# GpSimd's order in the steady passes: a k*v product ahead of the first sum, behind a wait for the gated attention rows

## The chip, the core and the metric

The kernel runs on one core of a Trainium2 chip. The metric is device time in microseconds (us), median over runs. The core has TensorE (matrix products), VectorE, ScalarE and GpSimd (elementwise work, each with its own queue of instructions), and SyncE, which here only issues transfers. The engines wait for each other by semaphores.

## What is computed

Two layers follow one another. The first is a cross-attention over 64 sequences of 64 channels and 256 steps, with a batch normalisation. The second is a recurrent layer (time mixing with a per-channel state, then channel mixing). The change lies in the second. Its core, cut short:

```python
xn = _ln(x, ln1_w, ln1_b)
sx = _token_shift(xn, state[:, i1])
x5 = xn[:, :, None] + sx[:, :, None] * (maa_stack + xxx)     # five mixed inputs
w = jnp.exp(-jnp.exp(time_decay + jnp.tanh(x5[:, :, 1] @ decay_w1) @ decay_w2))
r, k, v = x5[:, :, 3] @ Wr.T, x5[:, :, 0] @ Wk.T, x5[:, :, 2] @ Wv.T
g = jax.nn.silu(x5[:, :, 4] @ Wg.T)
def step(s, rkvw):                       # 64 steps, per head an 8 x 8 state
    a = k_t[:, :, :, None] * v_t[:, :, None, :]
    out = jnp.einsum('bhk,bhkd->bhd', r_t, u * a + s)
    return (a + w_t[:, :, :, None] * s, out)
x = x + (groupnorm(att) * gn_w + gn_b) * g @ Wo.T
xn2 = _ln(x, ln2_w, ln2_b); sx2 = _token_shift(xn2, state[:, i0])
kk = jnp.square(jax.nn.relu((xn2 + sx2 * ffn_maa_k) @ ffn_Wk.T))
x = x + jax.nn.sigmoid((xn2 + sx2 * ffn_maa_r) @ ffn_Wr.T) * (kk @ ffn_Wv.T)
```

## The kernel before

Everything is float32. The second layer works through 8 chunks (`CHUNKS`) of 8 sequences, 512 tokens each. Each engine has its own program, written out by hand; a pass of an engine is a call of its `body(n, p)`. A steady pass `n` does three things at once: the late part of chunk n-1 (`c_...`: group norm, output projection, second layernorm, channel mixing), the state part of chunk n (`b_...`) and the early part of chunk n+1 (`a_...`: shift, mixed inputs, projections). Before the steady passes 1 to 6 lie a filling and a first pass, behind them a last pass and a draining one. Passes 1 to 4 are a loop of two bodies (an odd and an even one) whose semaphore values come from registers. Passes 5 and 6 are written out with constants, and pass 6 has no `z_add`.

The state part handles two halves of the channels (h = 0, 1), each in two parts (q = 0, 1) of 512 x 4 columns. For each (h, q):
- k*v (`b_kv`) is formed in the state buffer `st[q]`: by GpSimd for (0, 0), (0, 1) and (1, 0) (L656), by VectorE for (1, 1) (L1446). It reads `vb[h]`, into which SyncE has spread v by eight transfers (L601).
- VectorE runs four scans over it (L1459, decay `w` in PSUM) and then the product with r (L1464), which writes over `vb` and frees `st[q]`. TensorE sums the product up (L858).

Buffers `st[0]` and `st[1]` take turns, so the k*v of (1, 0) can start as soon as the product of (0, 0) is done (semaphore `prod_ready`).

The mixed inputs go through three engines: TensorE makes the modulation (L816, L821), VectorE multiplies it by the shift into `x5` (`a_mod`, L1419), and GpSimd adds xn (`add_x(n + 1, j)`, L683). Then TensorE projects: j = 0 feeds the decay (`a_dec1`, L830 and L832), j = 1 the values (L793 on `ps_a`), j = 2, 3, 4 the keys, receptances and gates. `add_x` waits for the second channel half of its modulation (`mod_ready`).

VectorE's steady pass, as far as it matters here: scans and product of (0, 0), bonus and shift, the group norm of chunk n-1 (`c_gn`: L1523 twice, then the gated rows `ag`, L1527 twice, each of which raises `ag_ready`), the modulations 0 and 1 (L1419 four times), scans and product of (0, 1), the moments of x1 (`c_x1`, L1391 to L1397), scans and product of (1, 0), the second shift with the key mix (`c_shift`, L1537, L1541), further modulations and the k*v of (1, 1), scans and product of (1, 1), and the output gate (L1551).

GpSimd's steady pass: first tokens (`prev`), `add_x` 0, k*v (1, 0), `z_add` (a transfer from memory that adds, L662), `add_x` 1, a square root of the second layernorm (`rstd`, L638, L640), `add_x` 2 and 3, `rstd` of the first layernorm, k*v (0, 0) of the next chunk, `add_x` 4, k*v (0, 1), and the output's transfer (L669).

Of the kernel before, what the change touches and what calls it, by code (L numbers as in the profile page):

```python
# [46 lines left out]
def wait(eng, sem, value):  # L47

    if isinstance(value, int) and value <= 0:
        return  # L50
    eng.wait_ge(sem, value)
# [374 lines left out]
def rwkv(nc, sem, t, d, out):  # L426
# [30 lines left out]
    att_copied, att_sq, var_ln, gn_rstd, gn_scaled, ag_ready = sem("att_copied"), sem("att_squared"), sem("var_ln"), sem("gn_rstd"), sem("att_scaled"), sem("att_gated")  # L457
# [40 lines left out]
    with ctx:  # L498
# [57 lines left out]
        def wide(ap):  # L556

            return bt(ap).rearrange("p b (a t) -> p a b t", a=1).broadcast_to([P, 4, NB, L])
# [15 lines left out]
        def kv_at(n, h, q):  # L574

            if (h, q) in KV_BY_POOL:
                return kv_pool, n * len(KV_BY_POOL) + KV_BY_POOL.index((h, q)) + 1
            return kv_vector, n * len(KV_BY_VECTOR) + KV_BY_VECTOR.index((h, q)) + 1
# [56 lines left out]
        def _(pool):  # L635
            def rstd(n, var_sem, sem_out, src, dst):
                pool.wait_ge(var_sem, n * 2 + 2)
                nc.gpsimd.tensor_tensor(dst[:, 0, :], src[:, 0, :], t["mhalf"][:, :], ALU.pow).then_inc(sem_out, 1)  # L638
                pool.wait_ge(sem_out, n * 2 + 1)
                nc.gpsimd.tensor_tensor(dst[:, 1, :], src[:, 1, :], dst[:, 0, :], ALU.mult).then_inc(sem_out, 1)  # L640

            def prev(n, shift_sem, sem_out, src, dst):

                wait(pool, shift_sem, n)
                for c in range(EC):
                    nc.gpsimd.tensor_copy(dst[:, NB * c:NB * c + NB, 0], src[:, c, bass.ds(n * NB, NB)]).then_inc(sem_out, 1)  # L646

            def b_kv(n, p, h, q):

                pool.wait_ge(v_spread[h], n * 16 * S + 16 * S)  # L650
                pool.wait_ge(k_ready, n * 2 + h + 1)
                src = vb[h][:, q:S:2, :].rearrange("p e (b t) -> p e b t", t=L)
                wait(pool, prod_ready, n * 4 + 2 * h + q - 1)
                if isinstance(n, int) and n == 0 and (h, q) == (0, 1):
                    pool.wait_ge(kv_pool, 1)
                nc.gpsimd.tensor_tensor(st[q][:, :, :, 1:L], src[:, :, :, 0:L - 1], wide(k[p][h][:, :])[:, :, :, 0:L - 1],  # L656
                                        ALU.mult).then_inc(kv_at(n, h, q)[0], 1)

            def z_add(n):

                pool.wait_ge(x_biased, n)
                pool.dma_start(wyz[:, bass.ds(n * TILES, TILES), :], d["x"][bass.ds(n * TILES, TILES)].rearrange("a p f -> p a f"),  # L662
                               accum_op=ALU.add).then_inc(z_ready, 16)

            def add_out(n):

                pool.wait_ge(y_mid, n * 2 + 4)
                pool.wait_ge(x1_stored, n * 16 + 16)
                pool.dma_start(out[bass.ds(n * TILES, TILES)].rearrange("a p f -> p a f"), y, accum_op=ALU.add).then_inc(stored, 16)  # L669

            def last_rstd2(i):
# [3 lines left out]
                pool.wait_ge(last_ln, 2 * i + 1)  # L675
                nc.gpsimd.tensor_tensor(rs2[:, 1, cut], ve2[:, 1, cut], rs2[:, 0, cut], ALU.mult).then_inc(last_ln, 1)

            def hold(n):
                pool.wait_ge(bonus_ready, n * 2 + 2)

            def add_x(n, j):
                pool.wait_ge(mod_ready, n * 10 + MOD_ORDER.index(f"w{j}b") + 1)
                nc.gpsimd.tensor_tensor(x5[j % 2][:, :, :], x5[j % 2][:, :, :], xn[:, :, 1:L1], ALU.add).then_inc(x5_ready, 1)  # L683
# [8 lines left out]
            def first_pass(n, p):  # L692
                q = 1 - p
                prev(n + 1, sx_ready, xprev, t["prev1"], xn)
                hold(n)
                b_kv(n, p, 1, 0)
                add_x(n + 1, 0)
                add_x(n + 1, 1)
                z_add(n + 2)
                add_x(n + 1, 2)  # L700
                add_x(n + 1, 3)
                b_kv(n + 1, q, 0, 0)
                add_x(n + 1, 4)
                rstd(n + 2, ln1_var, ln1_rstd, ve1, rs1)
                b_kv(n + 1, q, 0, 1)

            def body(n, p, z=True):
                q = 1 - p
                prev(n - 1, sx2_ready, xprev2, t["prev0"], xn2)
                prev(n + 1, sx_ready, xprev, t["prev1"], xn)  # L710
                add_x(n + 1, 0)
                b_kv(n, p, 1, 0)
                if z:
                    z_add(n + 2)
                add_x(n + 1, 1)
                rstd(n - 1, ln2_var, ln2_rstd, ve2, rs2)
                add_x(n + 1, 2)
                add_x(n + 1, 3)
                if z:
                    rstd(n + 2, ln1_var, ln1_rstd, ve1, rs1)  # L720
                b_kv(n + 1, q, 0, 0)
                add_x(n + 1, 4)
                b_kv(n + 1, q, 0, 1)
                add_out(n - 1)
# [23 lines left out]
            with pool.Fori(1, CHUNKS - 4, 2) as n:  # L748
                body(n, 1)
                body(n + 1, 0)  # L750
            body(CHUNKS - 3, 1)
            body(CHUNKS - 2, 0, z=False)
            last_pass(CHUNKS - 1, 1)
# [1020 lines left out]
```

## Time and profile before

| | us |
|---|---|
| median of 3 runs | 692.4 (690.88 to 697.16) |
| the profiled execution, its own time | 689.89 |
| its span, first to last instruction | 688.0 |
| TensorE busy (matrix products) | 613.5 (89%) |
| VectorE busy | 574.1 (83%) |
| ScalarE busy | 390.5 (57%) |
| GpSimd busy | 294.1 (43%) |
| chain that ended last: PE, DVE, issue, POOL | 29%, 17%, 11%, 7% |

In the profile TensorE is called PE (PEld its weight loads), VectorE DVE, ScalarE ACT, GpSimd POOL and SyncE SP; POOLq is GpSimd's sequencer. All times in rows are microseconds from the start of the span unless marked ns. Busy time is an average over the attention layer (up to about 150 us), the passes and the ends. The steady passes run from about 270 to 626 us.

### The profile page before, as it was taken

To read this page: it belongs to the slowest core of one execution; us is meant where nothing else is said; L and a number is where in the kernel's file an instruction comes from. 1 tells how busy PE (TensorE), PEld (TensorE's weight loads), DVE (VectorE), ACT (ScalarE), POOL (GpSimd) and SP (SyncE) were. 2 spreads that over 40 slices of the span, in tenths; PEclk is the share of its full clock that TensorE was granted. 3 is DMA by queue.
4 is the path that set the end of the run, shared out by engine and by line. 5 is a ranking of instruction groups with operands and counts; after the bars stand their busy time and mean duration, and the time that the engine had idled before them with its cause. 6 is when DMAs were issued, how large, how long until landed. Compare 5 with 4: busy or idle time off the path is not lost.

```text
span 688.0 us, 9610 instructions
## 1 busy us (share of the span) xinstructions
PE 613.5 (89%) x2694; PEld 332.2 (48%) x2694; DVE 574.1 (83%) x902; ACT 390.5 (57%) x933; POOL 294.1 (43%) x210
## 2 busy tenths in 40 slices
PE   8999999979787859899899989989988998995896
PEld 5666666647232224354445435344543534443475
DVE  2999999973568898978997997899799789959944
ACT  3888888853443354567365455737546464353343
POOL 1111363002035293475639428464851946590020
PEclk9999999999999999999999999999999999998699
DMA  2343222201270841456267055526706540670020
GB/s 68 121 124 105 83 72 61 83 13 31 77 168 0 154 92 31 80 135 124 31 153 143 10 106 131 99 30 152 152 4 127 131 74 4 149 153 30 0 31 30
DMA packets 42444, 57.87 MB, mean 84 GB/s; under 512 B 4978, under 2 KB 25106, under 8 KB 42418
## 3 DMA queue, kind: packets, MB, share of 16 engines
q1 hardware_dynamic: 33008, 46.77, 29.6%
q0 software_dynamic: 9104, 10.77, 8.9%
q8 instruction: 11, 0.18, 0.1%
q14 instruction: 15, 0.12, 0.1%
q10 hardware_dynamic: 306, 0.02, 0.0%
HBM read 16.13 MB, written 7.86 MB: 35 GB/s over the span
## 4 chain that ended last, share of the span: by engine, by line
PE 29%; DVE 17%; issue 11%; POOL 7%; ACT 4%; DMA 1%; SPq 1%; DVEq 0%; POOLq 0%; ACTq 0%
PE ps_a L793 9%; DVE state L1459 8%; PE ps_c L878 6%; PE ps_c L793 3%; POOL x L683 2%; POOL state L656 2%; DVE vb L1464 2%; PE ps_att L858 2%; DVE x L1419 2%; PE ps_a L816 1%; PE ps_a L821 1%; DVE sx L1537 1%; DMA vb<-v 1%; PE ps_c L931 1%; POOL xn L646 1%
## 5 line engine op out<-in xcount | busy, mean ns | idle before, releaser
L683 POOL TENSOR_TENSOR x<-x,xn 128x1024 f32<-128x1024 f32 x35 | 86.2, 2471 | 151.0 <-DVE x L1419 151.0
L1459 DVE TENSOR_TENSOR_SCAN state<-ps_w,state 128x512 f32<-128x512 f32 x128 | 145.8, 1200 | 0.2
L793 PE MATMUL ps_a<-x,wsq 128*128 128x512 f32 x256 | 119.3, 610 | 10.1 <-POOL x L683 7.5
L656 POOL TENSOR_TENSOR state<-vb,k 128x2016 f32<-128x2016 f32 x23 | 105.3, 4577 | 27.0 <-DVE state L1446 10.4
L1464 DVE TENSOR_TENSOR vb<-state,r 128x2048 f32<-128x2048 f32 x32 | 86.1, 2692 | 1.7
L793 PEld LDWEIGHTS ps_a<-x,wsq 128*128 128x128 f32 x256 | 48.5, 195 | 68.9 <-issue 59.4
L1419 DVE SCALAR_TENSOR_TENSOR x<-ps_a,vec,sx 128x512 f32<-128x512 f32 x80 | 56.2, 745 | 27.7 <-PE ps_a L816 15.9
L310 ACT ACTIVATE probs<-ps_f,negmax 128x256 f32<-128x256 f32 x128 | 59.0, 473 | 1.9 <-DVE negmax L364 1.1
L816 PE MATMUL ps_a<-mix_t,w 64*128 64x512 f32 x128 | 47.6, 634 | 9.8 <-ACT mix_t L1161 7.1
L1117 ACT ACTIVATE zn<-wyz,rs 128x256 f32 (+1 forms) x60 | 31.1, 594 | 22.5 <-POOL rs L640 22.5
L374 DVE TENSOR_SCALAR probs<-probs,rowinv 128x256 f32<-128x256 f32 x128 | 41.8, 369 | 2.2
L1213 ACT ACTIVATE wyz<-ps_c 128x512 f32 (+1 forms) x14 | 8.4, 597 | 60.0 <-PE ps_c L892 60.0
L858 PE MATMUL ps_att<-vb,pick 128*32 128x512 f32 x256 | 35.0, 619 | 8.3 <-DVE vb L1464 8.3
L364 DVE TENSOR_REDUCE negmax<-ps_f 128x2 f32<-128x512 f32 x64 | 40.9, 681 | 0.9 <-PE ps_f L226 0.9
L249 PE MATMUL ps_av<-probsT,gz 128*64 128x256 f32 x256 | 34.7, 388 | 3.8 <-issue 2.4
L226 PE MATMUL ps_f<-thph 32*128 32x256 f32 x256 | 36.2, 400 | 0.5 <-ACT thph L318 0.5
L236 PE MATMUL ps_t<-cst,probs 128*128 128x128 f32 x256 | 35.6, 280 | 0.7 <-DVE probs L374 0.7
L1184 ACT ACTIVATE r<-ps_a 128x512 f32<-128x512 f32 x16 | 9.4, 595 | 46.7 <-PE ps_a L793 46.7
L793 PE MATMUL ps_c<-zn,wsq 128*128 128x512 f32 x56 | 28.6, 657 | 6.6 <-DVE zn L1541 6.6
L816 PEld LDWEIGHTS ps_a<-mix_t,w 64*128 64x128 f32 x128 | 14.3, 185 | 41.1 <-issue 15.5
L236 PEld LDWEIGHTS ps_t<-cst,probs 128*128 128x128 f32 x256 | 27.3, 140 | 12.1 <-DVE probs L374 11.4
L638 POOL TENSOR_TENSOR rs<-ve,mhalf 128x4 f32<-128x4 f32 x15 | 16.4, 1095 | 38.8 <-ACT ve L1129 20.8
(213 smaller groups left out, 1259.3 us busy)
## 6 DMA issues: line engine op xcount, KB each, us to landing
vb<-v SPq DMA_DIRECT2D x120, 256.0 KB, 5.5
x<-in_x SPq DMA_DIRECT2D x32, 128.0 KB, 2.1
c<-in_ctx SPq DMA_DIRECT2D x32, 128.0 KB, 2.3
wyz<-in_x POOLq DMA_DIRECT2D x7, 512.0 KB, 5.9
out<-wyz SPq DMA_DIRECT2D x7, 512.0 KB, 7.4
out<-sx POOLq DMA_DIRECT2D x7, 512.0 KB, 6.4
vb<-v SPq DMA_DIRECT2D x16, 128.0 KB, 2.4
wsq<-in_wsq POOLq DMA_DIRECT2D x7, 256.0 KB, 3.2
```

The lines of the kernel that those rows point to most:

```text
L236: mm = nc.tensor.transpose(ps_t[e][:, T * j + P * i:T * j + P * i + P], pr[2 * p + e][:, i, P * j:P * j + P], ident)
L310: mm = nc.scalar.activation(pr[b][:, i, :], score_bank(k, e)[:, T * i:T * i + T], ACT.Exp, bias=nm[b][:, i:i + 1], accum_out=rs[b][:, i:i ...
L374: nc.vector.tensor_scalar(pr[b][:, i, :], pr[b][:, i, :], ri[b][:, i:i + 1], None, ALU.mult).then_inc(s_scl, 1)
L656: nc.gpsimd.tensor_tensor(st[q][:, :, :, 1:L], src[:, :, :, 0:L - 1], wide(k[p][h][:, :])[:, :, :, 0:L - 1], ALU.mult).then_inc(kv_at(n, h ...
L683: nc.gpsimd.tensor_tensor(x5[j % 2][:, :, :], x5[j % 2][:, :, :], xn[:, :, 1:L1], ALU.add).then_inc(x5_ready, 1)
L793: mm = nc.tensor.matmul(bank[:, :], wsq[:, weight, c, P * o:P * o + P], src(c), start=(c == 0), stop=(c == EC - 1))
L816: nc.tensor.matmul(bank[:, :], t["w2"][rows, i % 2, P * c:P * c + P], t1[rows, :], start=True, stop=True).then_inc(a_done, 1)
L858: mm = nc.tensor.matmul(att[32 * i:32 * i + 32, :], pick[:, q, :], vb[h][:, 2 * i + q, :], start=(q == 0), stop=False)
L878: mm = nc.tensor.matmul(bank[:, E * m:E * m + E], lhs(c)[:, lo:lo + P], wsq[:, weight, c, :], start=(c == 0), stop=(c == EC - 1))
L1419: nc.vector.scalar_tensor_tensor(x5[j % 2][:, NB * c:NB * c + NB, :], bt(ab(name)[:, :]), col(STK0 + MIX_OF[j], c), sx[:, NB * c:NB * c + ...
L1459: nc.vector.tensor_tensor_scan(row, w[h][:, :], row, 0.0, ALU.mult, ALU.add).then_inc(scanned, 1)
L1464: nc.vector.tensor_tensor(src, st[q][:, :, :, :], wide(r[p][h][:, :]), ALU.mult).then_inc(prod_ready, 1)
```

## The change

GpSimd's steady pass gets a wait for both gated rows of chunk n-1, and behind it the k*v (1, 0), which moves ahead of the first sum. All other work and every other engine's program stay as they are.

```diff
+            def hold_gated(n):
+                pool.wait_ge(ag_ready, n * 2 + 2)
...
                 prev(n - 1, sx2_ready, xprev2, t["prev0"], xn2)
                 prev(n + 1, sx_ready, xprev, t["prev1"], xn)
+                hold_gated(n - 1)
+                b_kv(n, p, 1, 0)
                 add_x(n + 1, 0)
-                b_kv(n, p, 1, 0)
                 if z:
                     z_add(n + 2)
                 add_x(n + 1, 1)
```

GpSimd's instructions in the odd body of the loop, from the last copy of first tokens on. `x_0<-x_0,xn` is the first sum, `state<-vb,k` the k*v; ISA and REGISTER_ALU rows are steps of the sequencer that work out semaphore values, waits among them. Before:

```order
L646 COPY xn<-prev 128x8
L682 ISA
L683 TENSOR_TENSOR x_0<-x_0,xn 128x1024
L650 ISA
L651 ISA
L51 ISA
L656 TENSOR_TENSOR state<-vb,k 128x32x63
L661 REGISTER_ALU
L662 ISA
L662 DMA wyz<-in_x 128x4x256
```

And with the change:

```order
L646 COPY xn<-prev 128x8
L679 ISA
L650 ISA
L651 ISA
L51 ISA
L656 TENSOR_TENSOR state<-vb,k 128x32x63
L685 ISA
L686 TENSOR_TENSOR x_0<-x_0,xn 128x1024
L661 REGISTER_ALU
L662 ISA
L662 DMA wyz<-in_x 128x4x256
```

The k*v and its three steps have moved ahead of the first sum, and one step (L679) for the new wait stands before them. The three lines added above push `add_x` from L683 to L686.

The second place is the sixth steady pass, where no transfer stands between the sums. GpSimd before:

```order
L646 COPY xn<-prev 128x8 x4
L683 TENSOR_TENSOR x_0<-x_0,xn 128x1024
L656 TENSOR_TENSOR state<-vb,k 128x32x63
L683 TENSOR_TENSOR x_1<-x_1,xn 128x1024
L638 TENSOR_TENSOR rs<-ve,mhalf 128x4
```

And with the change:

```order
L646 COPY xn<-prev 128x8 x4
L656 TENSOR_TENSOR state<-vb,k 128x32x63
L686 TENSOR_TENSOR x_0<-x_0,xn 128x1024
L686 TENSOR_TENSOR x_1<-x_1,xn 128x1024
L638 TENSOR_TENSOR rs<-ve,mhalf 128x4
```

Here the two sums now follow one another directly, where the k*v lay between them.

## Rows read from the trace of the kernel before

**Rows 1.** Table by stage, one steady pass: us, then busy us (instructions), clock, DMA share, GB/s.

```profile
core 0: us, PE busy (x) PEld busy (x) DVE busy (x) ACT busy (x) POOL busy (x), PEclk, DMA share, GB/s
447.73:506.89 59.16, 54.87 (x196) 26.77 (x192) 52.87 (x62) 34.08 (x72) 34.83 (x19) 1.00 0.49 98
```

**Rows 2.** Timeline of VectorE, 444 to 468: start, us, engine, line, operation [idle before].

```profile
444.26 1.41 DVE L1527 SCALAR_TENSOR_TENSOR ag<-ag,gn_eh,gate 128x512 f32<-128x512 f32 x2
445.58 2.72 DVE L1419 SCALAR_TENSOR_TENSOR x<-ps_a,vec,sx 128x512 f32<-128x512 f32 x4
448.22 4.56 DVE L1459 TENSOR_TENSOR_SCAN state<-ps_w,state 128x512 f32<-128x512 f32 x4
452.81 3.67 DVE L1464 TENSOR_TENSOR vb<-state,r 128x2048 f32<-128x2048 f32 x1
...
458.53 4.55 DVE L1459 TENSOR_TENSOR_SCAN state<-ps_w,state 128x512 f32<-128x512 f32 x4
...
466.58 1.41 DVE L1541 SCALAR_TENSOR_TENSOR zn<-sx,vec,xn 128x512 f32<-128x512 f32 x2
```

**Rows 3.** Timeline of TensorE, same pass: decay, reduction, values, keys.

```profile
453.81 0.64 PE L832 MATMUL ps_a<-x,dw 128*64 128x512 f32 x1
...
455.15 0.59 PE L832 MATMUL ps_a<-x,dw 128*64 128x512 f32 x1
456.53 1.07 PE L858 MATMUL ps_att<-vb,pick 128*32 128x512 f32 x8 [0.79 <-DVE vb L1464]
458.65 3.70 PE L793 MATMUL ps_a<-x,wsq 128*128 128x512 f32 x8 [1.05 <-POOL x L683]
...
468.05 3.70 PE L793 MATMUL ps_c<-zn,wsq 128*128 128x512 f32 x8 [0.94 <-DVE zn L1541]
```

**Rows 4.** Timelines of GpSimd and VectorE in the first pass, at 221.

```profile
221.51 1.31 POOL L662 DMA_DIRECT2D wyz<-in_x  x1
...
222.35 2.29 DVE L1464 TENSOR_TENSOR vb<-state,r 128x2048 f32<-128x2048 f32 x1
```

**Rows 5.** Timeline of GpSimd, 447 to 459, steady pass.

```profile
447.73 2.17 POOL L683 TENSOR_TENSOR x<-x,xn 128x1024 f32<-128x1024 f32 x1 [10.40 <-DVE x L1419]
449.86 4.47 POOL L656 TENSOR_TENSOR state<-vb,k 128x2016 f32<-128x2016 f32 x1
454.28 1.30 POOL L662 DMA_DIRECT2D wyz<-in_x  x1
455.11 3.41 POOL L683 TENSOR_TENSOR x<-x,xn 128x1024 f32<-128x1024 f32 x1
```

**Rows 6.** Timeline, first and sixth steady pass: blocked products, gated rows, k*v.

```profile
275.31 3.68 DVE L1464 TENSOR_TENSOR vb<-state,r 128x2048 f32<-128x2048 f32 x1
...
562.66 1.41 DVE L1527 SCALAR_TENSOR_TENSOR ag<-ag,gn_eh,gate 128x512 f32<-128x512 f32 x2
...
568.26 4.49 POOL L656 TENSOR_TENSOR state<-vb,k 128x2016 f32<-128x2016 f32 x1
571.21 3.69 DVE L1464 TENSOR_TENSOR vb<-state,r 128x2048 f32<-128x2048 f32 x1
```

**Rows 7.** By line, GpSimd's sequencer: ns min/median/max, first and last start.

```profile
L650 POOLq FUSED_REGOPS  x6: 46/51/51, 270.2 to 479.0; - x6
...
L651 POOLq FUSED_REGOPS  x4: 37/40/43, 270.3 to 420.0; - x4
...
L51 POOLq FUSED_REGOPS  x4: 37/40/43, 270.4 to 420.0; - x4
```

**Rows 8.** Table by stage, columns as rows 1: the queues before the gated rows.

```profile
439.00:440.00 1.00, 1.00 (x4) 0.44 (x3) 1.00 (x2) 0.99 (x2) 0.00 (x0) 1.00 0.00 0
```

**Rows 9.** By line, 481 to 486: modulations beside a k*v, columns as rows 7.

```profile
L1419 DVE SCALAR_TENSOR_TENSOR x<-ps_a,vec,sx x2: 751/751/751, 482.0 to 482.8; 128x512 f32<-128x512 f32 x2
...
L656 POOL TENSOR_TENSOR state<-vb,k x1: 4495/4495/4495, 481.1 to 481.1; 128x2016 f32<-128x2016 f32 x1
```

**Rows 10.** Timeline of ScalarE, same steady pass: x1 and the decay.

```profile
454.01 0.60 ACT L1213 ACTIVATE wyz<-ps_c 128x512 f32 x1 [1.99 <-PE ps_c L892]
...
457.41 0.57 ACT L1174 ACTIVATE ps_w<-ps_w 128x504 f32<-128x504 f32 x1
```

## The prediction

> **What bounds the kernel now.** I read the table by stage first. A steady pass takes 59.16 us, with TensorE busy 54.87 and VectorE 52.87 of them at a granted clock of 1.00 [rows 1]: neither engine is full, so they must be waiting in turn, and an average doesn't say where. The pass that starts at 447.73 stands for all six steady ones (270.22, 329.40, 388.56, 447.73, 506.89, 566.13).
>
> Then I read VectorE's timeline of that pass [rows 2]. From the end of the gated rows (second L1527, 445.67) it has no idle time up to the shift of the second layernorm: four modulations, four scans, a product (L1464), moments, four scans, a product, the shift, and the key mix (L1541) at 466.58. The keys on TensorE (L793 ps_c, 468.05) wait 0.94 us for just that mix [rows 3]. After 468.05 TensorE has no idle time until the next pass's mixing. So the stretch 445.67 to 468.05 is VectorE's, and whatever VectorE loses in it lengthens the pass one for one.
>
> It does lose something. The product L1464 is asked for at 452.81 and takes 3.67 us [rows 2]; the same product in the pass before the steady ones takes 2.29 [rows 4]. GpSimd's timeline says why: its k*v (L656) runs from 449.86 to 454.33 [rows 5], and 454.33 + 2.29 is, within 0.15, the 456.48 at which the product ends. The product stands blocked for 1.38 us until the k*v is done. The effect runs both ways: the second sum (L683) is entered at 455.11 and takes 3.41 us rather than the first one's 2.17 [rows 5], because the product is still running. The blocked product is there in all six steady passes, at 3.67 to 3.69 us; the first starts at 275.31, the last at 571.21 [rows 6].
>
> The Trainium skill (SBUF — State Buffer, "SBUF: two separate sides") states the same as a lock: VectorE operations with two SBUF inputs and GpSimd operations that read SBUF hold one shared pair for the whole instruction, and the loser waits. By that rule the trace agrees (3.67 against 2.29).
>
> **What the change moves.** No work is added or removed. In GpSimd's steady pass the k*v of (1, 0) goes from behind the first sum to ahead of it, and starts behind a wait for both gated rows.
>
> *When the k*v starts.* The last gated row ends at 445.67 [rows 2]. The first sum starts 0.08 us after the modulation that releases it (third L1419, 447.65, against 447.73) [rows 5]. Behind the new wait the loop has up to three more register and wait steps (L650, L651, L51), which the sequencer used to run while the sum was busy. They start 0.1 us apart (270.2, 270.3, 270.4) [rows 7]. So the start is 445.67 + 0.08 + 0.3 = 446.05. In the even body of the loop it is 0.1 less, and in the passes written out less still.
>
> *Its other inputs.* k is copied and the product that frees its buffer is done before the pass's head. The spread v is the last to land. The DMA queues are silent by 439 [rows 8], 6.6 us before the gated rows end, so the earlier start meets no transfer. SP's and POOL's own queues are passed by nothing: z_add keeps its place behind the k*v and the first sum.
>
> *What stands beside it.* 446.05 + 4.47 = 450.52. Under it lie the modulations and the scans. Both read one operand from PSUM. In this same pass scans already run beside a k*v without loss, and two modulations beside the k*v of 481.1 took 0.751 us each against a usual 0.74 to 0.75 [rows 9]. I price this at nothing. The bound from above is a full block of the three modulations that are left when the k*v starts, some 4 us a pass, and I see no row that points there.
>
> *The first sum.* 450.48 + 2.17 = 452.65. That is 2.7 us later than before (449.90). Its reader, the decay matmuls, starts on TensorE behind the attention output at 453.81 [rows 3], so 1.15 us are left.
>
> *The product.* VectorE asks for it at 452.81, 0.16 us behind the end of the first sum. It starts at once and ends at 455.10 and not 456.48. That is the gain: **1.38 us**. If the release steps take longer than 0.54 us in all, each 0.1 us more costs 0.1 us of it. A bound on the loss: with the release 1.9 us late nothing would be left.
>
> *z_add and the second sum.* The DMA is issued at 452.61. The operation behind it is entered 0.83 us later (454.28 to 455.11 [rows 5]), so at 453.44, and VectorE's product has begun 0.63 us before. The second sum waits for it and ends at 455.10 + 2.04 = 457.14 (before: 456.48 + 2.04 = 458.52). The first pass shows just this order already: z_add at 221.51, the product at 222.35 with 2.29 us [rows 4], and a sum after z_add.
>
> *Does everything behind it follow?* The value projection on TensorE waited 1.05 us for the second sum, and the reduction of the product (L858) 0.79 us for it [rows 3]; both are released 1.38 us earlier, TensorE being free from 455.74. The moments need x1, whose second copy on ScalarE ends at 454.61 [rows 10], under the new 455.10: this cover shrinks from 1.8 to 0.4 us, but holds. The second scans need w: ScalarE's column waits for the product, and its second exponential ended 1.50 us after the product did (457.98) [rows 10], so now 456.60, and the scans start at 458.53 - 1.38 = 457.15. The normalisation hangs on GpSimd's rstd, which starts behind the moments and the second sum, both 1.38 earlier. So the keys start 1.38 us earlier, and with them the rest of the pass. What TensorE has idle falls from 4.3 to about 2.9 us a pass.
>
> *The sixth steady pass has no z_add.* There the second sum follows the first at once. With the gated rows done at 564.07 the k*v runs from 564.15 to 568.63, the first sum to 570.78, the second from 570.74 to 572.90, and the product, asked for at 571.21, gets in after it, where it came in after the k*v at 572.75 before [rows 6]. No gain there, but a loss of 0.15.
>
> **Sum.** 5 x 1.38 - 0.15 = 6.75 us. The profiled execution's own time is 689.89 (span 688.0): 683.1. The median of the runs is 692.4, 2.5 above the profiled one, and I carry the difference over to it: 692.4 - 6.75 = **685.6 us**, 0.98% less.
>
> **The rivals.**
>
> *The gain is lost on the way* (15 in 100). The release takes up to 2 us, or x1 or w comes later than the moments or scans want them. For it: three covers (0.16, 0.4 and 0.55 us) are thin, and all would be used in every pass. Against: all three are distances within one pass that move together. Each has to slip by more than its cover first, and only the excess counts. Time: between 687.5 and 692.5, say 690.
>
> *The second sum gets in first* (8 in 100). If VectorE asks for the product more than 0.63 us later than forecast, or GpSimd reaches the second sum as much earlier, the sum runs and the product waits for all of it. Deciding point: 453.44 against 452.81. Then the product starts at 453.44 + 2.13 = 455.57 instead of 454.33, 1.24 us later than before. Five such passes and the sixth's 0.15 make +6.4, so 698.8 us. For it: the sixth pass does exactly this, for lack of z_add. What would cause it in the others is that the moved k*v slows the modulations by 0.63 us together. Against: the 0.751 us each beside a k*v [rows 9], and the first pass, where z_add gave the product its place. [...]
>
> *It changes nothing, since TensorE is the bound* (5 in 100). It is busy 54.87 of 59.16 us, and the gain could turn into other waits of its own. Then 692.4. Against: its waits for VectorE and GpSimd between 456 and 468 are the ones that shrink.
>
> *More than forecast* (4 in 100): 680 to 683, if the waits at the following pass's head shrink too. No row shows why they should.
>
> **How the numbers follow.** The forecast has 68 in 100, with a range of its own of 684 to 688. The range to 8 in 10 takes in most of the lost gain: 683 to 691. About 1% is what a measurement of this kernel can tell from no change, and that is 6.9 us here. The forecast, 6.75, stands just short of it: I give 0.33 of its 0.68 to over 1% faster, and with the last rival 0.37. Slower by over 1% is the second rival with a little beside: 0.09. The rest is 0.54.
>
> **What would show it.** L1464 at 2.29 us in five steady passes and about 3.8 in the sixth; GpSimd's k*v starting 0.2 to 0.4 us after the second L1527; the second sum still above 3 us, blocked by the product; TensorE's wait for the second sum at about 0.5 us; passes of 57.8 us, the sixth at 59.3. The forecast is wrong if L1419 exceeds 0.76 us beside the k*v, if L1464 keeps more than 3 us, or if the product is short and the pass still takes 59 us.

## The result and the profile after

The changed kernel is slower: 700.24 us median against 693.26 (18 runs each), ratio 1.0114 with a 95% interval of 1.0096 to 1.0133 (the two medians alone are 7.0 us or 1.0% apart). The forecast was 685.6. The profiled execution took 699.35, its span is 697.4.

The steady passes carry it. From the first z_add to the fifth, four passes, the kernel before took 236.67 us (59.17 a pass) and the changed one 242.95 (60.74). The tables by stage, before and after:

```profile
276.78:513.45 236.67, 219.49 (x771) 107.09 (x769) 211.61 (x245) 136.40 (x289) 139.30 (x73) 1.00 0.49 98
```

```profile
276.86:519.81 242.95, 220.71 (x768) 107.54 (x768) 217.86 (x245) 136.30 (x288) 136.37 (x73) 0.99 0.48 95
```

1.57 us more in each of five passes make 7.9, the 1.14% of the runs. The sixth pass adds almost nothing: from its product of (0, 1) to that of the last pass it is 55.72 us before (571.21 to 626.93) and 55.75 after (580.90 to 636.65). (The span shows 9.4. Of these 1.8 lie ahead of the steady passes, which the change doesn't touch: the k*v of the first pass starts at 214.21 and not 212.44. What made that difference no run shows. Behind the last pass's product 0.3 are won back.) VectorE's busy time rises by 6.25 us in this stretch, with the same 245 instructions.

The timeline of VectorE, fourth steady pass of the changed kernel (L1531 is the L1527 of before, L1423 its L1419, L1463 its L1459, L1468 its product L1464, all four lines further down):

```profile
451.00 1.41 DVE L1531 SCALAR_TENSOR_TENSOR ag<-ag,gn_eh,gate 128x512 f32<-128x512 f32 x2
452.33 2.72 DVE L1423 SCALAR_TENSOR_TENSOR x<-ps_a,vec,sx 128x512 f32<-128x512 f32 x4
454.97 4.55 DVE L1463 TENSOR_TENSOR_SCAN state<-ps_w,state 128x512 f32<-128x512 f32 x4
459.56 5.34 DVE L1468 TENSOR_TENSOR vb<-state,r 128x2048 f32<-128x2048 f32 x1
```

And GpSimd's, beside it:

```profile
452.65 4.47 POOL L656 TENSOR_TENSOR state<-vb,k 128x2016 f32<-128x2016 f32 x1 [8.59 <-DVE ag L1531]
457.10 2.17 POOL L686 TENSOR_TENSOR x<-x,xn 128x1024 f32<-128x1024 f32 x1
459.22 1.30 POOL L662 DMA_DIRECT2D wyz<-in_x  x1
460.05 2.69 POOL L686 TENSOR_TENSOR x<-x,xn 128x1024 f32<-128x1024 f32 x1
```

Up to the product all goes as forecast. The modulations and scans beside the k*v take 2.72 and 4.55 us, as in [rows 2], and the first sum is done at 459.27, 0.29 us before VectorE asks for the product. But the product takes 5.34 us instead of 2.29. It ends at 464.90, which is the second sum's end (462.74) plus 2.16. So it stood behind z_add *and* the second sum, although the sum's row begins 0.49 us later than its own. And the sum didn't run from its entry: its 2.69 us are the usual 2.17 counted from z_add's end, 460.52 ([rows 5] had it waiting for the product instead). The product waits 3.05 us instead of the 1.38 of before: 1.67 us worse a pass, of which 1.57 reach the pass. VectorE's step behind the moments (L1396 before, L1400 now) gives 0.12 of it back. It waits for a sum that is still running on GpSimd: before, it took 0.29 us and ended with the second sum; now the sum is long done and it takes 0.17:

```profile
458.25 0.29 DVE L1396 TENSOR_SCALAR ve<-mv 128x4 f32<-128x4 f32 x1
```

```profile
466.68 0.17 DVE L1400 TENSOR_SCALAR ve<-mv 128x4 f32<-128x4 f32 x1
```

On TensorE the wait for the product grows from the 0.79 us of [rows 3] to 2.46, while the values no longer wait for the second sum:

```profile
464.95 1.07 PE L862 MATMUL ps_att<-vb,pick 128*32 128x512 f32 x8 [2.46 <-DVE vb L1468]
465.95 3.70 PE L797 MATMUL ps_a<-x,wsq 128*128 128x512 f32 x8
```

All five passes with a z_add show the same. The product is asked for 0.23, 0.34, 0.21, 0.34 and 0.50 us behind z_add's start and takes 5.46, 5.33, 5.45, 5.34 and 5.17. The sixth pass has no z_add, and there it takes the 3.83 us of the forecast:

```profile
580.90 3.83 DVE L1468 TENSOR_TENSOR vb<-state,r 128x2048 f32<-128x2048 f32 x1
```

```profile
578.28 4.32 POOL L686 TENSOR_TENSOR x<-x,xn 128x1024 f32<-128x1024 f32 x2
```

So z_add is what differs. Two theories offered themselves: z_add's own work holds up the product (A), or the sum queued behind z_add gets the pair first although its row begins later (B). In the diffs below `hold_product(n)` waits for `prod_ready` at n * 4 + 2, the end of the product of (0, 1), and `hold_scans(n)` for `scanned` at n * 16 + 8, its last scan. All diffs are against the changed kernel.

### The profile page after: what moved, and what is told of

Same layout as the page of the kernel before. It is cut to its first block, busy times and chain, and to the rows that moved or that the text cites. A ratio compares the mean times of both kernels' runs of the same rounds, so it can differ in the third digit from the quotient of the medians.

```text
span 697.4 us, 9614 instructions
## 1 busy us (share of the span) xinstructions
PE 617.8 (89%) x2694; PEld 334.7 (48%) x2694; DVE 582.0 (83%) x902; ACT 390.5 (56%) x933; POOL 288.4 (41%) x210
## 4 chain that ended last, share of the span: by engine, by line
PE 33%; DVE 18%; issue 9%; ACT 5%; POOL 3%; DMA 1%; SPq 1%; DVEq 0%; POOLq 0%; ACTq 0%
PE ps_a L797 11%; DVE state L1463 8%; PE ps_c L882 7%; PE ps_c L797 3%; DVE vb L1468 3%; PE ps_att L862 2%; POOL x L686 2%; DVE x L1423 2%; PE ps_a L825 2%; PE ps_a L820 1%; DVE sx L1541 1%; ACT sq L1209 1%; DMA vb<-v 1%; PE ps_c L935 1%; DVE st L1395 1%
## 5 line engine op out<-in xcount | busy, mean ns | idle before, releaser
L1463 DVE TENSOR_TENSOR_SCAN state<-ps_w,state 128x512 f32<-128x512 f32 x128 | 145.8, 1201 | 0.2
L797 PE MATMUL ps_a<-x,wsq 128*128 128x512 f32 x256 | 121.9, 620 | 3.9 <-DVE x L1427 2.6
L686 POOL TENSOR_TENSOR x<-x,xn 128x1024 f32<-128x1024 f32 x35 | 80.5, 2310 | 89.2 <-DVE x L1423 89.2
L1468 DVE TENSOR_TENSOR vb<-state,r 128x2048 f32<-128x2048 f32 x32 | 94.7, 2958 | 1.6
L1423 DVE SCALAR_TENSOR_TENSOR x<-ps_a,vec,sx 128x512 f32<-128x512 f32 x80 | 56.2, 745 | 27.7 <-PE ps_a L820 15.9
```

What stands on the lines that cost most here:

```text
L797: mm = nc.tensor.matmul(bank[:, :], wsq[:, weight, c, P * o:P * o + P], src(c), start=(c == 0), stop=(c == EC - 1))
L1423: nc.vector.scalar_tensor_tensor(x5[j % 2][:, NB * c:NB * c + NB, :], bt(ab(name)[:, :]), col(STK0 + MIX_OF[j], c), sx[:, NB * c:NB * c + ...
L1463: nc.vector.tensor_tensor_scan(row, w[h][:, :], row, 0.0, ALU.mult, ALU.add).then_inc(scanned, 1)
L1468: nc.vector.tensor_tensor(src, st[q][:, :, :, :], wide(r[p][h][:, :]), ALU.mult).then_inc(prod_ready, 1)
```

## Experiments: is it z_add or the sum, and is the gain there

**x1: the sum held back behind z_add.**

```diff
                 if z:
                     z_add(n + 2)
+                hold_product(n)
                 add_x(n + 1, 1)
```

> One edit to the changed kernel: between z_add and the second sum GpSimd waits for the product of (0, 1). Theory A (z_add's own work on GpSimd blocks the product that is asked for 0.34 us behind its start): the product still starts late, when z_add is done, so L1468 takes 2.29 plus up to 1.0, that is 2.9 to 3.3 us, and the kernel lies near the one before, 689 to 694. Theory B (z_add blocks nothing; the sum queued behind it takes the pair although the product was asked for first): with the sum held back the product takes 2.29 us in all six passes, and the kernel is 5 to 8 us below the one before, about 687.

Measured: 684.26 us, ratio to the kernel before 0.9867 (0.9827 to 0.9906): 9.0 us less, where 5 to 8 were expected. Timelines of GpSimd and VectorE in x1:

```profile
450.55 1.30 POOL L662 DMA_DIRECT2D wyz<-in_x  x1
450.88 2.29 DVE L1472 TENSOR_TENSOR vb<-state,r 128x2048 f32<-128x2048 f32 x1
...
453.34 2.17 POOL L689 TENSOR_TENSOR x<-x,xn 128x1024 f32<-128x1024 f32 x1 [1.49 <-DVE vb L1472]
```

The product is asked for 0.33 us behind z_add's start, as in the changed kernel, and runs its 2.29 us straight through it, in all six passes. A transfer alone does not block the product, so theory A falls. What blocked it was the sum. A pass takes 57.97 us.

**x2: the sum first, then z_add.**

```diff
+                hold_product(n)
+                add_x(n + 1, 1)
                 if z:
                     z_add(n + 2)
-                add_x(n + 1, 1)
```

> The changed kernel with GpSimd's wait for the product of (0, 1) behind the first sum, and then the second sum ahead of z_add. Both theories: nothing of GpSimd runs when VectorE asks for the product, so L1468 takes 2.29 us in all six passes, the second sum runs its 2.17 us right behind it and ends within 0.2 us of the forecast's 457.14, and each pass takes 57.8 to 58.0 us instead of 59.17: 6 x 1.2 to 1.38 below the kernel before, some 685 to 686. If the step of the prediction that says that a product started on time shortens the pass is itself wrong, the passes stay at 59 us.

Measured: 686.75 us, 0.9897 (0.9858 to 0.9936). The product takes 2.29 us in all six passes, and a pass takes 58.41, 0.4 more than forecast. z_add now stands ahead of the square root of the second layernorm, whose own row grows from 1.03 us to 1.56 behind it:

```profile
457.93 1.31 POOL L662 DMA_DIRECT2D wyz<-in_x  x1
458.75 1.56 POOL L638 TENSOR_TENSOR rs<-ve,mhalf 128x4 f32<-128x4 f32 x1
```

The step "a product on time shortens the pass" holds, and a transfer costs what stands behind it on GpSimd half a microsecond more than its neighbour's entry suggests. That this delay is what makes the pass longer than x1's fits, but no run takes it by itself.

## Experiments: when the sum gets the pair

**x3 and x4: the offset between product and z_add shifted by tiny fills.**

```diff
+                for _ in range(6):                    # x3, VectorE, ahead of the product of (0, 1)
+                    nc.vector.memset(idle[:, _:_ + 1], 0.0)
...
+                for _ in range(5):                    # x4, GpSimd, ahead of z_add
+                    nc.gpsimd.memset(idle[:, _:_ + 1], 0.0)
```

> The changed kernel with six one-column fills on VectorE ahead of the product of (0, 1), some 0.3 to 0.4 us, so that it is asked for about 0.7 us behind z_add's start instead of 0.34, still ahead of the second sum's entry (0.83). Theory A: the first part of z_add is what blocks, a product asked for at 0.62 behind the output's transfer was not blocked in the kernel before, so L1468 takes 2.29 us here and a slower VectorE makes the kernel faster: about 687 to 690. Theory B: asked for later, the product loses to the sum as before (about 5 us), and the kernel is at 700 or above.

> The changed kernel with five one-column fills on GpSimd ahead of z_add, about 0.6 us, so that the product of (0, 1) is asked for before z_add starts and not behind it. Theory A: the product has the pair first, takes 2.29 us in five passes, and the kernel is at about 686 to 688. Theory B: the product loses to whatever sum GpSimd has queued; then L1468 stays near 5 us and the kernel at 700.

Measured: x3 698.77 us (1.0084, 1.0059 to 1.011), x4 695.62 (1.0041, 1.0011 to 1.0071). The fills were far shorter than I took them for. x3's moved the product by 0.05 us, which shows nothing new: all five passes lose, at offsets of 0.26 to 0.55 us. x4's took 0.2 us instead of 0.6, and this miss was the most telling run. Its product is asked for 0.09, 0.19, 0.07, 0.19 and 0.36 us behind z_add's start. Timelines, first and third pass of x4:

```profile
278.48 1.33 POOL L663 DMA_DIRECT2D wyz<-in_x  x1
```

```profile
278.57 5.61 DVE L1471 TENSOR_TENSOR vb<-state,r 128x2048 f32<-128x2048 f32 x1
```

```profile
400.38 1.29 POOL L663 DMA_DIRECT2D wyz<-in_x  x1
401.20 3.58 POOL L687 TENSOR_TENSOR x<-x,xn 128x1024 f32<-128x1024 f32 x1
```

```profile
400.45 2.29 DVE L1471 TENSOR_TENSOR vb<-state,r 128x2048 f32<-128x2048 f32 x1
```

At 0.09 us the product loses, at 0.07 it wins; each is one pass of one execution. The pass behind the win takes 57.66 us (400.38 to 458.04), the one ahead of it 60.99 (339.39 to 400.38). Which passes won in the other runs no record shows. The profiled one, at 699.83, is among the slowest of ten with a median of 695.62. The spread of the ten, 692.55 to 699.95, says nothing of a race: x14 below, whose product wins in every pass of its profile, spreads from 682.08 to 690.65.

**x5 and x6: who is issued when.**

```diff
                     z_add(n + 2)
+                hold_scans(n)                         # x5
                 add_x(n + 1, 1)
...
+                nc.gpsimd.memset(idle[:, :], 0.0)     # x6, idle is 128x512
                 if z:
                     z_add(n + 2)
```

> As x1, but the wait between z_add and the second sum is for the last scan of part (0, 1) and not for the product: the sum is let go at the moment at which VectorE asks for the product, and no longer sits issued behind z_add. Theory C (a sum that is already issued claims the shared pair when z_add ahead of it starts, ahead of its own recorded entry): let go only 0.3 us behind z_add's start and at or just behind the product's request, the sum loses, L1468 takes 2.29 us, the sum runs behind it, 683 to 686. Theory D (whatever sum of GpSimd is pending wins against a product asked for while z_add runs): L1468 stays near 5.3 us and the kernel near 700.

> The changed kernel with one fill of 128x512 on GpSimd (some 0.5 us) ahead of z_add, so that VectorE asks for the product about 0.15 us before z_add starts; z_add and the sum are issued ahead just as in the changed kernel. Theory C: the claim is made at z_add's start, so the product is first: 2.29 us in five passes, 685 to 689. Theory D: L1468 stays near 5 us and the kernel near 700. Between them (2.4 to 4 us in L1468) would mean that the fill holds the pair as well.

Measured: x5 685.02 us (0.9902, 0.9869 to 0.9934), x6 683.49 (0.9878, 0.9836 to 0.992). In x5 the product takes 2.29 us in all six passes. The product's offset behind z_add is the same as in the changed kernel; only the sum is let go later, by the last scan, about 0.3 us behind z_add's start. Timelines of GpSimd and VectorE in x5:

```profile
450.42 1.30 POOL L662 DMA_DIRECT2D wyz<-in_x  x1
450.76 2.29 DVE L1472 TENSOR_TENSOR vb<-state,r 128x2048 f32<-128x2048 f32 x1
451.24 3.85 POOL L689 TENSOR_TENSOR x<-x,xn 128x1024 f32<-128x1024 f32 x1
```

The sum's entry again lies about 0.8 us behind z_add's start, just as where it won (460.05), but now it is the sum that waits. Its recorded entry says nothing about who comes first. In x6 GpSimd does 0.5 us more, the product is asked for 0.12 to 0.25 us before z_add (0.04 behind it in the fifth pass), it wins all five, and the kernel with more work is 2.4% faster than the changed one.

x5's pass is also 0.3 us shorter than x1's, 57.68 against 57.97, although the product takes 2.29 us in both. The step behind the moments shows why (L1404 in both, L1400 in the changed kernel). In x1 the sum is let go only by the product's end and runs until 455.51; the step takes 0.59 us and ends at 455.54. In x5 the sum follows the product at once and is done at 455.09; the step takes 0.29 us and ends at 455.12. First x1, then x5:

```profile
454.95 0.59 DVE L1404 TENSOR_SCALAR ve<-mv 128x4 f32<-128x4 f32 x1
```

```profile
454.83 0.29 DVE L1404 TENSOR_SCALAR ve<-mv 128x4 f32<-128x4 f32 x1
```

So an issued sum has its claim at most 0.09 us behind z_add's start. That it can be issued long before is in GpSimd's sequencer rows. The step that stands ahead of the second sum in the changed kernel's fourth pass runs at 455.2, while the k*v is still busy (the row's other step, at 468.1, belongs to the third sum):

```profile
L685 POOLq ALU_OP  x2: 32/32/32, 455.2 to 468.1; - x2
```

**x10: a fill in z_add's place.**

```diff
-                if z:
-                    z_add(n + 2)
+                nc.gpsimd.memset(idle[:, :], 0.0)     # 128x900
                 add_x(n + 1, 1)
                 rstd(n - 1, ln2_var, ln2_rstd, ve2, rs2)
+                if z:
+                    z_add(n + 2)
```

> The changed kernel with z_add behind the square root and, in its place between the two sums, a fill of 128x900 on GpSimd (about 0.9 us, close to the 0.83 between z_add's start and the entry of the sum). The second sum is issued ahead as in the changed kernel, and VectorE asks for the product some 0.35 us behind the fill's start. Theory C1 (the early claim belongs to a transfer): the product has the pair, 2.29 us, the kernel at 684 to 686. Theory C2 (an issued sum claims the pair from behind any operation of GpSimd that is running): L1468 takes about 0.5 + 2.17 + 2.15 = 4.8 us in five passes and the kernel is at 697 to 700.

Measured: 682.85 us, 0.9864 (0.9831 to 0.9898). The timelines of x10:

```profile
449.83 0.84 POOL L718 MEMSET idle<- 128x900 f32 x1
450.16 2.29 DVE L1470 TENSOR_TENSOR vb<-state,r 128x2048 f32<-128x2048 f32 x1
450.64 3.86 POOL L687 TENSOR_TENSOR x<-x,xn 128x1024 f32<-128x1024 f32 x1
```

The sum is issued ahead exactly as in the changed kernel, the operation ahead of it is as long as the 0.83 us between z_add and the sum's entry, and the product is asked for 0.33 us into it. It wins. The early claim belongs to the transfer (theory C1); an issued sum behind a fill doesn't have it. Nor has one behind a k*v, as the sixth pass of the kernel before shows. There the product has been asked for at 571.21, the k*v ends at 572.75, and the product, not the sum issued behind the k*v, comes next: it ends at 574.90 [rows 6], and the sum waits for it:

```profile
572.70 4.23 POOL L683 TENSOR_TENSOR x<-x,xn 128x1024 f32<-128x1024 f32 x1
```

**x12 and x14: a copy between z_add and the sum.**

```diff
                     z_add(n + 2)
+                nc.gpsimd.tensor_copy(idle[:, 0:4], t["mhalf"][:, :])
+                hold_scans(n)                         # x14 only
                 add_x(n + 1, 1)
```

> The changed kernel with one tiny copy on GpSimd (128x4) between z_add and the second sum, all three issued ahead, so that the operation right behind the transfer is a copy with one input and not a sum with two. The product is asked for 0.2 to 0.5 us behind z_add's start, as in the changed kernel. Theory E (only the operation right behind a transfer claims early, and a copy, as behind the output's transfer in the kernel before, where a product asked for 0.62 us behind it was not blocked, does not claim against the product): L1468 takes 2.29 us in five passes, the kernel is at 684 to 686. Theory F (a sum issued anywhere behind a running transfer claims the pair): L1468 stays at 5.2 to 5.5 us and the kernel at 699 to 701.

> As x12 (z_add with a tiny copy issued right behind it), but the second sum is let go only by the last scan of part (0, 1). Theory J (the early claim comes with any operation issued behind a transfer, the copy too, and the product then waits until GpSimd's queue runs dry): the product waits for the transfer and the copy, L1468 at 3.2 to 3.6 us or, if the sum slips in as well, at 5.4. Theory K (only the sum claims, even with the copy ahead of it): L1468 at 2.29 us in all passes, the kernel at 684 to 686.

Measured: x12 699.74 us (1.0104, 1.0084 to 1.0124), x14 683.87 (0.9897, 0.9867 to 0.9928). Timelines of GpSimd and VectorE, first x12, then x14:

```profile
458.12 1.28 POOL L663 DMA_DIRECT2D wyz<-in_x  x1
458.45 5.44 DVE L1470 TENSOR_TENSOR vb<-state,r 128x2048 f32<-128x2048 f32 x1
458.92 0.68 POOL L720 COPY idle<-mhalf 128x4 f32<-128x4 f32 x1
459.07 2.66 POOL L687 TENSOR_TENSOR x<-x,xn 128x1024 f32<-128x1024 f32 x1
```

```profile
448.51 1.32 POOL L663 DMA_DIRECT2D wyz<-in_x  x1
448.86 2.29 DVE L1474 TENSOR_TENSOR vb<-state,r 128x2048 f32<-128x2048 f32 x1
449.31 1.88 POOL L723 COPY idle<-mhalf 128x4 f32<-128x4 f32 x1
```

With the sum issued behind transfer and copy the product loses to both. With only the copy behind the transfer the product wins and the copy waits for it. Theory E falls: a copy in between is no guard. Theory K stands: it takes an issued sum. Whether that is for the sum's second input or for its size (128x1024 against 128x4) no run shows.

**x13: the product later still.**

```diff
+                nc.vector.memset(idle[:, :], 0.0)     # VectorE, 128x340, ahead of the product of (0, 1)
```

> The changed kernel with one fill of 128x340 on VectorE ahead of the product of (0, 1), about 0.3 us, so that it is asked for some 0.5 us (passes 1 and 3), 0.6 us (2 and 4) and 0.8 us (5) behind z_add's start; the second sum is entered at 0.83. Theory H (the product loses only in a first part of the transfer, up to between 0.55 and 0.61): passes 2, 4 and 5 have L1468 at 2.29 us, 1 and 3 at about 5.2; the kernel is at 690 to 693, faster than the changed kernel although VectorE does more. Theory I (with a sum issued behind the transfer the product loses until the sum's entry): all five at 4.8 to 5.2 us, and 700.

Measured: 701.9 us, 1.0125 (1.0077 to 1.0174). At offsets of 0.57, 0.70, 0.58, 0.71 and 0.86 us the product takes 5.10, 4.94, 5.09, 4.96 and 4.81. The second pass, GpSimd and VectorE:

```profile
342.99 1.29 POOL L663 DMA_DIRECT2D wyz<-in_x  x1
343.81 2.67 POOL L687 TENSOR_TENSOR x<-x,xn 128x1024 f32<-128x1024 f32 x1
```

```profile
343.69 4.94 DVE L1471 TENSOR_TENSOR vb<-state,r 128x2048 f32<-128x2048 f32 x1
```

It loses at every offset: theory I, and no window that closes at 0.6. (The fifth, at 0.86, is asked for 0.04 us behind the sum's entry and would lose by that alone.) The case of before that suggested such a window, 0.62 us behind the output's transfer, had copies behind it and no sum, which is x14's case.

## Experiments: the parts of the change and the better order

**x7: no wait for the gated rows; x8: that wait alone.**

```diff
-                hold_gated(n - 1)                     # x7
...
                 hold_gated(n - 1)                     # x8: the order of before behind it
-                b_kv(n, p, 1, 0)
                 add_x(n + 1, 0)
+                b_kv(n, p, 1, 0)
```

> The changed kernel without its wait for the gated rows: the k*v still stands ahead of the first sum, but starts as soon as the spread v has landed, at about 438.9 in the times of the kernel before. VectorE's mixes (L1413, two SBUF inputs) and its group norm (L1527, L1531) are asked for between 438.7 and 445.7. If the pair is held for a whole instruction, one mix or the first group-norm operation waits for the k*v, 0.5 to 4 us a pass, and the passes take 60 to 63 us: 695 to 715. If the wait for the gated rows is not needed, the passes are no longer than the changed kernel's 60.7.

> The kernel before with the new wait alone, its order unchanged: the first sum waits for its modulation anyway, 2 us behind the gated rows, so the wait costs nothing: L1468 at 3.68 us in six passes as before, the same time within 0.3%. Anything else would mean that the wait itself, and not the order, does part of the damage.

Measured: x7 714.52 us, 1.0312 (1.0269 to 1.0355); x8 692.69, 1.0002 (0.9976 to 1.0029). Two of x8's passes take 59.16 and 59.18 us, as before. The two others take 59.83 and 59.90, with a granted clock of 0.97 and TensorE 1.6 us busier; the product takes 3.67 to 3.74 us in all. The wait costs nothing by itself, and without it the kernel is 3% slower than before. x7's profiled execution took 723.97 us, so only who waits for whom is read from it. Timelines of GpSimd and VectorE:

```profile
456.21 4.46 POOL L656 TENSOR_TENSOR state<-vb,k 128x2016 f32<-128x2016 f32 x1
```

```profile
456.35 5.40 DVE L1409 TENSOR_TENSOR sx<-xn 128x1024 f32<-128x1024 f32 x1 [0.28 <-POOL xn L646]
```

The operation that waits is the shift (1.23 us otherwise), not a mix or the group norm as I had expected. It reads SBUF twice and stands behind the whole k*v, on the way to the mixing.

**x11: the second sum right behind the first.**

```diff
+                add_x(n + 1, 1)
                 if z:
                     z_add(n + 2)
-                add_x(n + 1, 1)
```

> The changed kernel with the second sum right behind the first and z_add behind it: all six passes then look like the changed kernel's sixth one. The second sum starts about 0.3 us before the product is asked for, so L1468 takes 3.7 to 3.9 us. Each pass is 0.15 us longer than before: 693 to 695. If z_add were not what doubles the loss in the changed kernel, this one would be at 700 too.

Measured: 693.7 us, 1.0049 (1.0023 to 1.0074), L1468 at 3.84 to 4.13 us, a pass at 59.42, 0.25 above the 59.17 of before. Without z_add between the sums the change costs 0.25 us a pass, with it 1.57.

**x9: the order that the runs pointed to.**

```diff
                 add_x(n + 1, 0)
-                if z:
-                    z_add(n + 2)
+                hold_scans(n)
                 add_x(n + 1, 1)
                 rstd(n - 1, ln2_var, ln2_rstd, ve2, rs2)
+                if z:
+                    z_add(n + 2)
```

> The best order that the runs point to: wait for the gated rows, k*v, first sum, wait for the last scan of part (0, 1), second sum, square root of the second layernorm, and only then z_add, in GpSimd's idle time. Theory C (an issued sum claims the pair ahead of its recorded entry only from behind z_add): here nothing of GpSimd claims the pair before VectorE asks for the product, so L1468 takes 2.29 us in all six passes, the sum runs right behind it, passes take 57.6 to 57.7 us, the sixth too: 6 x 1.5 = 9 below the kernel before, 682.5 to 684.5. If the release of the second sum at the last scan is early enough to beat the product now that z_add is gone, L1468 takes 4.4 us in the passes and the kernel is at 695 or above.

Measured: 684.57 us, 0.9917 (0.9885 to 0.9949), the product at 2.29 us in all six passes, a pass at 57.66. Its table by stage, to be read beside [rows 1]:

```profile
383.19:440.85 57.66, 54.78 (x192) 26.77 (x192) 51.36 (x62) 34.08 (x72) 36.11 (x18) 1.00 0.50 100
```

VectorE is 1.5 us less busy than in [rows 1], TensorE as busy as before. x1, x5, x6, x9, x10 and x14 lie at 682.9 to 685.0 us, their intervals overlap, and all are faster than the kernel before and the changed one. x9 is no better than the rest: its passes came out as expected, but its median lies only 6.4 us below the 691.0 measured for the kernel before together with it, where 9 were expected. Its profiled execution, 681.7, is 8.2 below that of the kernel before; its seven runs spread up to 690.63. Of them x1 is the smallest edit: the change as it was made, and one wait ahead of the second sum, for 0.9867.

## Why the prediction was wrong, step by step

*What bounds the pass*: right. The stretch from the gated rows to the key mix is VectorE's, and a product freed of its wait shortens the pass. In x5, x6, x9 and x10 the passes are 57.7 us on average; the sum had said 57.8. "One for one" holds only while the second sum still ends in time. In x1 the product gives back its 1.38 us and the pass only 1.2, since VectorE's step behind the moments waits for the sum. In x2 it is 0.76. This wait of VectorE the prediction didn't have.

*The k*v's start*: right, a little late. Said was 0.38 us behind the gated rows, it is 0.24 (452.65 against 452.41).

*What stands beside the k*v*: right. L1423 took 739 to 752 ns over all its 80 instructions, and the scans 4.55 us for four.

*The first sum*: right. It ends 0.29 us before the product is asked for; 0.16 was said. The decay matmuls didn't wait for it.

*"The operation behind it is entered 0.83 us later, so at 453.44, and VectorE's product has begun 0.63 us before"*: this is the step that failed. The entry is where the sum's row begins, 0.83 us behind z_add's, and that was measured right. But I took it for the moment at which the sum gets the shared pair. An issued sum has it at most 0.09 us behind the *transfer's* start (x4), with the product asked for at any later offset up to 0.86 losing (x13), and with the recorded entry in the same place when it loses (x5). The precedent that I leaned on, [rows 4], had nothing issued behind its z_add: there the next sum still waited for its modulation. That is x1's case. The row was right, and it was a precedent for another situation.

*The second rival* had the right outcome and sign: 698.8 us were said, 700.24 measured. Its condition, a product asked for 0.63 us later than forecast, did not come about, so its near hit is in part luck. It was given 8 in 100 because its deciding point was put at 453.44 with a cover of 0.63 us; the point that decides is z_add's start, and the product came 0.2 to 0.5 us too late for it. Its price was short as well. It let the sum run from its entry, while it runs from z_add's end, 0.47 us later: 1.24 us a pass were said, 1.57 measured.

*The sixth pass*: the product took 3.83 us against "about 3.8", which is right, but the pass lost 0.03 us and not 0.15. The product ends 0.14 us later, and the step behind the moments, which no longer meets the sum, gives 0.12 of it back (0.17 us instead of 0.29).

*The sum*: 5 x 1.38 was the gain of a kernel in which the sum is not issued behind z_add. The kernel in question pays 5 x 1.57 instead. The difference is 14.75 us, and between 685.6 and 700.24 lie 14.6. The agreement is closer than the medians allow: the kernel before took 692.4 over the three runs that the forecast stood on and 693.26 over eighteen.

## What to carry to other kernels

Where two engines share something that is held for a whole instruction, the order of the rows' starts doesn't say who gets it. Look for what is already *issued* on the other engine, above all behind a transfer, and hold the queued operation back with a semaphore that your own instruction's predecessor raises (here the last scan). A precedent in a trace counts only if the queue behind it was as full as it will be in the new order. And where a cover is a few tenths of a microsecond and losing it costs several, secure the order with a wait, or take the loss as likely.

## What the runs showed of the hardware

- A two-input sum on GpSimd that stands issued behind a transfer of GpSimd's own queue keeps VectorE's product out from the transfer's start (from 0.07 to 0.09 us behind it, x4) to the sum's end, though its own 2.17 us begin only when the transfer's 1.30 are over. A VectorE product with two SBUF inputs then waits up to 3.3 us. A sum behind a fill of 0.84 us has no such claim (x10), nor has a copy behind a transfer (x14). What in the engine causes it no run shows.
- A product that already waits when GpSimd's k*v ends is served before the next issued sum ([rows 6], sixth pass, sum entered at 572.70), so waiting products are not passed over in general.
- A VectorE `tensor_scalar` of 128x4 with a single SBUF input waits for a running GpSimd sum as well. It takes 0.17 us alone (changed kernel), 0.29 in the kernel before and 0.59 in x1, and ends 0.02 to 0.03 us behind the sum. The moments ahead of it don't wait: three take 1.06 us beside the sum (x1) and without it (changed kernel).
- A transfer's work on GpSimd was neither slowed by a running product nor slowed it: 1.28 to 1.37 us in every kernel, and 2.29 for the product (x1).
- The Trainium skill (SBUF — State Buffer, "SBUF: two separate sides") says that whoever of the two starts first has the pair. The runs agree where a k*v has started and the product (3.67 us) or the shift (5.40, x7) comes later. A GpSimd fill that starts 0.33 us ahead of the product holds nothing up (x10). For a sum behind a transfer "starts" has to be read as the transfer's start: in the changed kernel's fourth pass the sum's own row begins 0.49 us behind the product's, and it still wins.
- One-column fills, issued in a row, cost 0.01 us each on VectorE and 0.04 on GpSimd, not the 0.06 and 0.10 that the row of a single one lasts.
